# Two convolutions placed among the projection groups, with reordered work at three other places, in a one-core attention and FFN kernel

## The chip, the cores and the metric

The kernel runs on one core of one Trainium2 chip. The metric is device time in microseconds (us), the median of three runs. The core has a matrix engine (TensorE, PE in the profile; its weight loads are PEld), VectorE (DVE), ScalarE (ACT), GpSimd (POOL) and SyncE (SP), which here only issues DMAs. All operands come through SBUF, and matmul results land in PSUM, which has eight banks of 128 partitions x 512 float32.

## The reference

The input x has 32 batches of 64 channels x 1024. The reference computes, with everything in float32:

```python
x = x + attn(cond(x))          # cond: per-batch 64x64 mixing; attn: 32 batches of 64 rows, 32 heads, causal, plus a 10-row adapter
x = x + ffn(conv(x))           # conv: grouped, 9 taps along the 1024 axis, plus a context bias per batch
# ffn: base = xf @ W_base.T + b_base; top-2 router over 8 experts; rank-16 LoRA part added to base
```

In the reference the rows of attn's output and of ffn's input are the 2048 pairs (batch, channel), each of 1024 values. W_proj (in attn) and W_base (in ffn) are 1024 x 1024.

## The kernel before

Every large product is made of three matmuls that add up to float32 precision: each operand is split into a high part (ACT writes it, rounded) and a low part (DVE: value minus high part), and the passes are high x high, high x low and low x high. What the text calls a form is one operand in both parts: `high(G, f)` on ACT, then `low(G, f)` on DVE.

**Attention.** There are 32 units: 8 groups g of 128 output channels, 4 units u of 512 rows in each; n = 4g + u. In `unit_step`, PE projects K, Q and V (72 matmuls of 128x512), computes the scores of the unit before (L867), transposes, and multiplies with the values (L892, L898). DVE does the softmax of the unit before and rotates K and then Q (L1322 to L1329). ACT copies rotated K to `kbd` (four copies, L1196), then, where u is 0, the adapter's `akv` (L1207), then `aT` (L1131) and `pT` (L1134). In 16 of the units a slice of the weight forms of the later products is prepared as well: DVE subtracts blocks of the weights (`prep_sums`, four operations, L1388), ACT writes high parts (`prep_high`), DVE low parts (`prep_low`), and SP stores them. In before `prep_sums` stands ahead of the rotation of K.

**Groups 0 to 15.** NJ is 8. Groups G = 0 to 7 are the projection (W_proj), groups 8 to 15 the FFN; each handles two pairs of batches (t = 0, 1; 128 rows each). A group multiplies 256 rows by a 1024 x 1024 matrix in blocks of 512 with seven products instead of eight: `product(G, i)`, i = 0 to 6, twelve matmuls of 128x512 each. The operand forms are called, in the order of i, A11, S1, A22, S2, A12, S4, S3; S1 to S4 are sums of blocks that DVE makes (`add_up`). The results lie in four banks (A, C, D, B), and DVE and ACT combine them:

- `first_share` (ACT) copies product 0 to s1; `shares` (DVE) makes w12 and u2 from s1 and x, and adds product 1;
- `share21` adds product 2, `share12` adds product 3 to w12 (L1458); product 6 waits for `share12`, since it writes into the same bank B;
- `out11`, `out12` and `row2` write the two output rows into x1 (L1467 in the projection, L1464 in the FFN).

Between the products PE is in program order, and so are the other engines: each wait on a semaphore holds up everything behind it on its engine. The order of the work is written out by hand. Around the first group: product(0, 0) to (0, 5) are interleaved with the tail of unit 31; DVE's order of group 0 is shares, share21, low(1, A11), low(1, A22), share12(0) and so on, and those low parts need the attention output of the next pairs, `raw` (SP's `load_y(1)`, L689). `load_y(1)` stands on SP behind the store of the last unit's y (`store_y`, L660), which needs ACT's copy of it (`y_copy`), which needs the previous store to have landed; that store is queued behind three loads of weight forms.

**The turn to the FFN.** x1 of a projection group is written to DRAM (`put_aside`, L756). `spread(p)` (SP, L766, eight DMAs) reads it back in another layout into one of two buffers x8[p % 2], `load_ctx(p)` (L707) fetches the context bias, `convolve(p)` (PE, L999, 32 matmuls of 128x128) convolves into PSUM banks 0 and 1 (`bConv`), and `convolved(p)` (DVE, L1499) adds the bias and writes `raw` for FFN group 8 + p // 2. So convolve(0) and convolve(1) stand in group 7, and spread(2) and spread(3) can only start when their buffers have been read, in group 7 as well; convolve(2) and (3) stand in group 8. `load_x(8, t)` (L697) reads x1 of the first pairs back from DRAM for group 8, and POOL adds the base bias (`add_bias`, L841) into xn, which `shares(8)` needs. In the same stretch ACT issues the loads of the seven FFN weight forms, 2 MB each.

In the FFN, `hidden(G)` (L1015, L1017) computes router logits and LoRA rows, DVE does the routing (L1519 to L1542), PE transposes (L1025) and adds the LoRA part (`low_rank`, L1030). At the end `row2(15)` is two DVE operations, and one DMA of 512 KB stores them.

## Time and profile before

| | |
|---|---|
| median of 3 runs | 1206.33 us (1205.59 to 1206.85) |
| the profiled execution's own time | 1210.87 us |
| its span | 1208.8 us |
| PE busy | 1157.4 us, 96% |
| DVE busy | 924.1 us, 76% |
| ACT busy | 441.4 us, 37% |
| POOL busy | 54.3 us, 4% |

The span is that of one execution under the hardware profiler, and all times of day below are counted from its start. It is 2.1 us shorter than the execution's own time, which counts what lies around it. Attention runs to about 750 us, the projection groups to about 923 us, the FFN groups to the end. PE's idle time is small in total, and the profile tells for each piece what ended it.

### The profile page before, as it was taken

What the parts mean: (1) busy time and instruction counts of PE and PEld (TensorE: products, weight loads), DVE (VectorE), ACT (ScalarE), POOL (GpSimd) and SP (SyncE); (2) the same over time, 40 slices, a digit from 0 to 9 for tenths busy, and PEclk for the clock granted to TensorE, in tenths of its full rate; (3) what the DMA queues carried; (4) which work ended last, traced back from release to release, by engine and by line L of the source; (5) the groups of instructions that cost most, each with busy time, mean ns of one, the idle gap of its engine ahead of it and who ended that gap; (6) DMA issues with size and microseconds to landing.
All of it is one profiled execution on the core that took longest, in us unless ns stands there. A gap on an engine that the chain in (4) does not pass through costs nothing.

```text
span 1208.8 us, 19539 instructions
## 1 busy us (share of the span) xinstructions
PE 1157.4 (96%) x7568; PEld 974.1 (81%) x7568; DVE 924.1 (76%) x1741; ACT 441.4 (37%) x815; POOL 54.3 (4%) x25
## 2 busy tenths in 40 slices
PE   6999999999999999999999999799999499999998
PEld 5988878878878878878888877688888388888887
DVE  5887878878787787787887888678776177777775
ACT  4435354453543544535435446223221012221110
POOL 1000000000000000000000000000000122111122
PEclk9999999999999999999999999899999799999999
DMA  7413123033042041141232386674459533432312
GB/s 232 146 54 128 31 87 132 27 97 122 28 132 87 28 157 62 51 133 62 87 98 85 96 341 250 256 213 141 174 214 386 155 107 110 109 110 92 91 54 88
DMA packets 99465, 152.68 MB, mean 126 GB/s; under 512 B 7322, under 2 KB 83630, under 8 KB 96686
## 3 DMA queue, kind: packets, MB, share of 16 engines
q1 hardware_dynamic: 98366, 136.75, 35.0%
q10 hardware_dynamic: 1008, 14.68, 3.2%
q8 instruction: 61, 1.00, 0.3%
q14 instruction: 30, 0.25, 0.1%
HBM read 96.87 MB, written 54.54 MB: 125 GB/s over the span
## 4 chain that ended last, share of the span: by engine, by line
PE 53%; DVE 23%; issue 9%; ACT 7%; DMA 5%; SPq 3%; POOL 0%; DVEq 0%; ACTq 0%
PE psum L984 23%; PE psum L915 14%; PE psum L999 5%; ACT a_kbd L1196 3%; DVE a_stat L1347 2%; DVE a_prob L1362 2%; DVE a_prob L1343 2%; DVE a_stat L1358 2%; PE psum L260 2%; PE psum L898 2%; PE psum L1030 2%; SPq L766 2%; PE psum L1015 2%; PE psum L867 1%; DVE f_prep_raw L1388 1%
## 5 line engine op out<-in xcount | busy, mean ns | idle before, releaser
L915 PE MATMUL psum<-z,w_hi 128*128 128x512 f32 x1536 | 481.8, 395 | 0.0
L915 PEld LDWEIGHTS psum<-z,w_hi 128*128 128x128 f32 x1536 | 283.0, 188 | 55.3
L915 PE MATMUL psum<-z,w_lo 128*128 128x512 f32 x768 | 300.3, 391 | 0.0
L984 PE MATMUL psum<-f_wform,f_act_hi 128*128 128x512 f32 x896 | 280.5, 394 | 7.3 <-DVE f_w L1458 7.3
L984 PEld LDWEIGHTS psum<-f_wform,f_act_hi 128*128 128x128 f32 x896 | 167.1, 189 | 41.5 <-issue 7.7
L1196 ACT ACTIVATE a_kbd<-a_kr 32x512 f32<-32x512 f32 x128 | 80.7, 631 | 260.4 <-DVE a_kr L1329 259.3
L984 PE MATMUL psum<-f_wform,f_act_lo 128*128 128x512 f32 x448 | 175.3, 391 | 0.0
L915 PEld LDWEIGHTS psum<-z,w_lo 128*128 128x128 f32 x768 | 144.4, 188 | 30.8
L984 PEld LDWEIGHTS psum<-f_wform,f_act_lo 128*128 128x128 f32 x448 | 84.7, 189 | 18.0
L841 POOL TENSOR_TENSOR f_xn<-f_x,_bbase 128x1024 f32<-128x1024 f32 x16 | 49.6, 3097 | 1072.0 <-DMA f_x<-x_scratch 1072.0
L1166 ACT ACTIVATE f_act_hi<-f_raw 128x512 fp32r<-128x512 f32 x56 | 33.3, 626 | 142.0 <-DVE f_raw L1499 93.4
L1166 ACT ACTIVATE f_act_hi<-f_act_sum 128x512 fp32r<-128x512 f32 x64 | 40.2, 633 | 112.3 <-DVE f_act_sum L1420 45.3
L1426 DVE TENSOR_TENSOR f_act_lo<-f_raw,f_act_hi 128x512 fp32r<-128x512 f32 x56 | 37.2, 688 | 46.9 <-ACT f_act_hi L1166 46.9
L1343 DVE TENSOR_TENSOR a_prob<-psum,a_mask 128x512 f32<-128x512 f32 x64 | 43.8, 685 | 34.7 <-PE psum L867 34.7
L1124 ACT ACTIVATE a_prob<-a_prob 128x512 f32<-128x512 f32 x64 | 40.5, 633 | 65.1 <-DVE a_prob L1349 64.7
L1243 ACT ACTIVATE a_vbd<-psum 64x256 f32<-64x256 f32 x128 | 48.6, 380 | 25.8 <-PE psum L927 24.7
L1426 DVE TENSOR_TENSOR f_act_lo<-f_act_sum,f_act_hi 128x512 fp32r<-128x512 f32 x64 | 44.0, 689 | 14.0 <-ACT f_act_hi L1166 13.8
L1324 DVE STREAM_SHUFFLE a_rot<-psum 128x512 f32<-128x512 f32 x64 | 47.0, 735 | 0.0
L1349 DVE TENSOR_TENSOR a_prob<-a_prob,a_stat 128x512 f32<-128x512 f32 x64 | 44.3, 692 | 2.2
L1327 DVE TENSOR_TENSOR a_rot<-a_rot,a_sin 128x512 f32<-128x512 f32 x64 | 44.3, 692 | 2.2
L1362 DVE TENSOR_TENSOR a_prob<-a_prob,a_stat 128x512 f32<-128x512 f32 x64 | 44.3, 692 | 2.2
L1347 DVE TENSOR_REDUCE a_stat<-a_prob 128x8 f32<-128x512 f32 x64 | 43.9, 687 | 2.2
(173 smaller groups left out, 1583.2 us busy)
## 6 DMA issues: line engine op xcount, KB each, us to landing
w_forms<-f_prep_lo SPq DMA_DIRECT2D x16, 896.0 KB, 4.7
f_wform<-w_forms SPq DMA_DIRECT2D x7, 2048.0 KB, 12.7
f_wform<-w_forms ACTq DMA_DIRECT2D x7, 2048.0 KB, 16.3
w_st<-in_wqkvT SPq DMA_DIRECT2D x7, 1536.0 KB, 7.0
w_forms<-f_prep_hi SPq DMA_DIRECT2D x16, 640.0 KB, 6.0
m_x<-in_x SPq DMA_DIRECT2D x16, 512.0 KB, 4.0
y_scratch<-a_ysb SPq DMA_DIRECT2D x32, 256.0 KB, 2.4
f_raw<-y_scratch SPq DMA_DIRECT2D x8, 1024.0 KB, 6.1
```

The lines of the kernel that those rows point to most:

```text
L841: pool.tensor_tensor(xn[:, t, :].rearrange("p (m q) -> p q m", q=PH), x1[:, t, :].rearrange("p (q m) -> p q m", q=PH), bbase[:].rearrange( ...
L915: mm = pe.matmul(dst, w[:, c, x, :], zs, start=(c == 0 and i == 0), stop=(c == KC - 1 and i == 2))
L984: mm = pe.matmul(prod_bank[i][:], a[:, c, :], wform[i][:, w, c, :], start=(i < 4 and c == 0 and n == 0), stop=(c == KH - 1 and n == 2), sk ...
L999: mm = pe.matmul(bConv[:, o:o + P], x8[p % 2][:, CONV * b + g, j:j + P], toep[:, g, j, :], start=(j == 0), stop=(j == 1))
L1166: act.activation(act_hi[f][:], src, ACT.Copy).then_inc(act_hi_set, 1)
L1196: cp = act.activation(kbd[HD * h:HD * (h + 1), :, h % 2 * NC:(h % 2 + 1) * NC], kr[HD * h:HD * (h + 1), :].rearrange("p (b k) -> p b k", k ...
L1243: cp = act.activation(vbd[NC * h:NC * (h + 1), :, b, :, HD * h:HD * (h + 1)], bV[NC * b:NC * (b + 1), :].rearrange("p (s a h e) -> p s a h ...
L1324: dve.stream_shuffle(rot[:], src[:], HALF_SWAP).then_inc(turned[x], 1)
L1343: dve.tensor_tensor(prob[t][:].rearrange("p (s h) k -> p s h k", h=2), score_slots[:, UP * t:UP * (t + 1), 0:2 * NC].rearrange("p s (h k) ...
L1347: dve.tensor_reduce(stat[:, t, 0, :], prob[t][:], AX, ALU.max).then_inc(row_max, 1)
L1362: dve.tensor_tensor(prob[t][:], prob[t][:], spread(t, 2), ALU.mult).then_inc(probs, 1)
L1426: dve.tensor_tensor(act_lo[f][:], src, act_hi[f][:].bitcast(F32), ALU.subtract).then_inc(act_set, 1)
```

## The change

It has five parts, apart from names.

1. `prep_sums` moves from ahead of K's rotation to between the rotations of K and Q.
2. First group: ACT makes four of the seven high forms of group 0 ahead of the copy of V, one behind it and two behind the exponentials of the last unit. DVE leaves low(0, S4) and low(0, S3) to after share21(0), and in group 0 share12, out11 and out12 stand ahead of the low parts of group 1. SP issues load_y(1) and load_x(1, 1) ahead of the last store_y; load_y(1) has an additional wait for the four forms that still read `raw`.
3. convolve(0) stands at the start of group 5 and convolve(1) at the start of group 6. Pair 1 uses PSUM banks 2 and 3, and both results stay in PSUM until group 7, where `convolved(0)` and `(1)` stand as before. spread(2) is issued in group 5 and spread(3) in group 6.
4. POOL's add_bias for group 8 reads x1 right after group 0 has written it, so x1 isn't read back from DRAM for group 8. The writes to x1 in group 1 wait for POOL.
5. In group 15 the two products into bank B and the LoRA part of bank B are split into halves of 256 columns (the second in bank 0), and so are share12 and row2, and the last store.

```diff
@@ SP
             def load_y(G):
                 wait(sp, act_summed, 4 * G)
+                if G == 1:
+                    sp.wait_ge(act_set, 4)
...
             def spread(p):
-                load_ctx(p)
+                if p not in (2, 3):
+                    load_ctx(p)
...
-            store_y(NG - 1, NU - 1)
             def proj_group(G):
...
                 load_y(G + 1)
                 load_x(G + 1, 1)
                 if G == 0:
+                    store_y(NG - 1, NU - 1)
                     sp.wait_ge(y_out, 16 * NG * NU)
...
                 load_x(G + 1, 0)
+                if G in (NJ - 3, NJ - 2):
+                    spread(G - NJ + 5)
             def turn_group():
                 put_aside(G - 1, 1)
-                spread(2)
-                spread(3)
+                load_ctx(2)
+                load_ctx(3)
                 put_aside(G, 0)
-                load_x(G + 1, 0)
                 put_aside(G, 1)
-                load_x(G + 1, 1)
@@ POOL
             def add_bias(G, t):
-                pool.wait_ge(x_in[t], 16 * (G + 1))
+                if G == NJ and t == 0:
+                    pool.wait_ge(row1_set, 2)
+                elif G == NJ:
+                    pool.wait_ge(row2_set, 1)
...
@@ PE
             def convolve(p):
+                if p == 1:
+                    pe.wait_ge(y_copied, NG * NU)
...
-                wait(pe, conv_set, 2 * p)
+                wait(pe, conv_set, 2 * p if p >= 2 else 0)
...
             def hidden(G):
-                    pe.wait_ge(y_copied, NG * NU)
+                    pe.wait_ge(conv_set, 4)
...
             def group(G):
+                if G in (NJ - 3, NJ - 2):
+                    convolve(G - NJ + 3)
                 for i in range(4):
                     product(G, i)
-                if NJ - 1 <= G < 2 * NJ - 1:
+                if NJ <= G < 2 * NJ - 1:
                     convolve(2 * (G - NJ + 1))
@@ ACT
                 if n == NG * NU - 1:
-                    for f in form_order(0):
+                    for f in form_order(0)[:4]:
                         high(0, f)
                 (copy of V)
+                if n == NG * NU - 1:
+                    high(0, S2)
...
             attend_exp(m)
+            high(0, S4)
+            high(0, S3)
             first_share(0)
@@ DVE
             def out_half(G, t, half, src, other):
                 if ffn(G):
+                    if G == NJ:
+                        dve.wait_ge(x1_out[t], 16 * NJ)
...
                 wait(dve, x1_out[t], 16 * G)
+                if G == 1:
+                    dve.wait_ge(xn_set, t + 1)
...
             def unit_step(g, u):
-                if prep_at(n) is not None:
-                    prep_sums(prep_at(n))
                 rotate(K_, bK, kr, n, ((kbd_set, n),), n)
+                if prep_at(n) is not None:
+                    prep_sums(prep_at(n))
                 rotate(Q_, bQ, qr, n, ((scores, 2 * n),), n)
```

DVE in an attention unit with a weight slice (unit 5 of 32). a_kr and a_qr are rotated K and Q, f_prep_raw the weight blocks. Before:

```order
L1379 CAST a_aprob<-a_aprob 128x2x4x20
L1388 TENSOR_TENSOR f_prep_raw<-f_prep_raw 128x256 x4
L1322 TENSOR_TENSOR a_kr<-psum,a_cos 128x512
L1324 STREAM_SHUFFLE a_rot<-psum 128x512
L1327 TENSOR_TENSOR a_rot<-a_rot,a_sin 128x512
L1329 TENSOR_TENSOR a_kr<-a_kr,a_rot 128x512
L1322 TENSOR_TENSOR a_qr<-psum,a_cos 128x512
```

and now:

```order
L1408 CAST a_aprob<-a_aprob 128x2x4x20
L1351 TENSOR_TENSOR a_kr<-psum,a_cos 128x512
L1353 STREAM_SHUFFLE a_rot<-psum 128x512
L1356 TENSOR_TENSOR a_rot<-a_rot,a_sin 128x512
L1358 TENSOR_TENSOR a_kr<-a_kr,a_rot 128x512
L1417 TENSOR_TENSOR f_prep_raw<-f_prep_raw 128x256 x4
L1351 TENSOR_TENSOR a_qr<-psum,a_cos 128x512
```

The four block sums have changed places with K's rotation; Q's rotation stands where it stood.

DVE in group 0, from share21(0) on. f_u_85 is u2, f_w_84 is w12, f_x_126 is x1, f_act_lo_64 to 70 are the low parts of A11, S1, A22, S2, A12, S4, S3, f_act_sum_73 is the sum S1. Before:

```order
L1453 TENSOR_TENSOR f_u_85<-psum,f_u_85 128x512
L1426 TENSOR_TENSOR f_act_lo_64<-f_raw,f_act_hi_56 128x512
L1426 TENSOR_TENSOR f_act_lo_66<-f_raw,f_act_hi_58 128x512
L1458 TENSOR_TENSOR f_w_84<-psum,f_w_84 128x512
L1412 TENSOR_TENSOR f_act_sum_73<-f_raw 128x512
L1415 TENSOR_TENSOR f_act_sum_75<-f_act_sum_73,f_raw 128x512
L1426 TENSOR_TENSOR f_act_lo_65<-f_act_sum_73,f_act_hi_57 128x512
L1467 TENSOR_TENSOR f_x_126<-psum,f_xt_81 128x64x8
```

and now:

```order
L1482 TENSOR_TENSOR f_u_85<-psum,f_u_85 128x512
L1455 TENSOR_TENSOR f_act_lo_69<-f_act_sum_77,f_act_hi_61 128x512
L1455 TENSOR_TENSOR f_act_lo_70<-f_act_sum_78,f_act_hi_62 128x512
L1492 TENSOR_TENSOR f_w_84<-psum,f_w_84 128x512
L1505 TENSOR_TENSOR f_x_126<-psum,f_xt_81 128x64x8
L1505 TENSOR_TENSOR f_x_126<-psum,f_w_84 128x64x8
L1455 TENSOR_TENSOR f_act_lo_64<-f_raw,f_act_hi_56 128x512
L1455 TENSOR_TENSOR f_act_lo_66<-f_raw,f_act_hi_58 128x512
L1441 TENSOR_TENSOR f_act_sum_73<-f_raw 128x512
L1444 TENSOR_TENSOR f_act_sum_75<-f_act_sum_73,f_raw 128x512
L1455 TENSOR_TENSOR f_act_lo_65<-f_act_sum_73,f_act_hi_57 128x512
```

share12(0) and both outputs of the first row have moved ahead of all work on the next pairs' `raw`, and the last two low parts of group 0 have moved in behind share21.

SP from group 6 to the first FFN group. _x_95 and f_x_next are the two convolution buffers, f_ctxb the context biases, x_scratch is x1 in DRAM. Before:

```order
L756 DMA x_scratch<-f_x_126 128x1024 x2
L707 DMA f_ctxb_134<-ctx_scratch 128x128
L766 DMA _x_95<-x_scratch 16x8x128 x8
L707 DMA f_ctxb_135<-ctx_scratch 128x128
L766 DMA f_x_next<-x_scratch 16x8x128 x8
L756 DMA x_scratch<-f_x_126 128x1024
L697 DMA f_x_126<-x_scratch 128x1024
L756 DMA x_scratch<-f_x_126 128x1024
L697 DMA f_x_126<-x_scratch 128x1024
```

and now:

```order
L771 DMA _x_95<-x_scratch 16x8x128 x8
L760 DMA x_scratch<-f_x_126 128x1024 x2
L694 DMA f_raw<-y_scratch 128x2x1024
L707 DMA f_xt_82<-in_x 128x1024
L707 DMA f_xt_81<-in_x 128x1024
L771 DMA f_x_next<-x_scratch 16x8x128 x8
L760 DMA x_scratch<-f_x_126 128x1024 x2
L711 DMA f_ctxb_134<-ctx_scratch 128x128
L711 DMA f_ctxb_135<-ctx_scratch 128x128
L760 DMA x_scratch<-f_x_126 128x1024 x2
```

The sixteen gathers for pairs 2 and 3 have moved one group and more ahead, and the two loads of x1 (L697) at this place are gone.

## Rows read from the trace of the kernel before

**Rows 1.** The page, parts 1 and 2: PE's row and its granted clock.

```profile
PE 1157.4 (96%) x7568; PEld 974.1 (81%) x7568; DVE 924.1 (76%) x1741; ACT 441.4 (37%) x815; POOL 54.3 (4%) x25
...
PEclk9999999999999999999999999899999799999999
```

**Rows 2.** Waits of PE: line, releaser, us in total, times, longest.

```profile
PE psum L999 <- DVE f_raw L1499: 10.9, 1, 10.9
PE psum L984 <- DVE f_w L1458: 7.3, 1, 7.3
PE psum L999 <- DMA _x<-x_scratch: 7.1, 1, 7.1
PE psum L898 <- ACT a_pT L1134: 4.6, 8, 0.6
...
PE psum L905 <- ACT a_akv L1207: 2.8, 7, 0.4
PE psum L892 <- ACT a_aT L1131: 2.8, 7, 0.6
...
PE psum L927 <- ACT a_vT L1232: 0.8, 1, 0.8
```

**Rows 3.** Timeline of PE, 908 to 972: start, duration, idle time before.

```profile
908.15 3.73 PE L999 MATMUL psum<-_toep,_x 128*128 128x128 f32 x32
...
945.72 5.89 PE L999 MATMUL psum<-_toep,_x 128*128 128x128 f32 x32 [7.14 <-DMA _x<-x_scratch]
...
965.25 6.33 PE L999 MATMUL psum<-_toep,f_x_next 128*128 128x128 f32 x32 [10.88 <-DVE f_raw L1499]
```

**Rows 4.** Timeline of SP and of DVE in the same stretch.

```profile
922.42 21.23 SPq L766 DMA_DIRECT2D f_x_next<-x_scratch  x8
...
956.63 0.69 DVE L1435 TENSOR_TENSOR f_w<-f_s,f_xn 128x512 f32<-128x512 f32 x1 [22.04 <-POOL f_xn L841]
```

**Rows 5.** The page, part 6: DMA issues, KB each, us to landing.

```profile
f_wform<-w_forms ACTq DMA_DIRECT2D x7, 2048.0 KB, 16.3
...
out<-f_x SPq DMA_DIRECT2D x16, 512.0 KB, 3.1
```

**Rows 6.** Timeline of PE, 777 to 784.

```profile
777.90 1.19 PE L984 MATMUL psum<-f_wform,f_act_hi 128*128 128x512 f32 x2 [7.29 <-DVE f_w L1458]
...
783.01 0.63 PE L984 MATMUL psum<-f_wform,f_act_hi 128*128 128x512 f32 x2
```

**Rows 7.** Chain of waits, 740 to 1209: start, duration, what.

```profile
751.09 16.89 DMA y_scratch<-a_ysb
...
769.17 5.95 DMA f_raw<-y_scratch
```

**Rows 8.** Chain of waits, 1190 to 1209: the last product.

```profile
1201.66 2.75 PE psum L984 x12
```

**Rows 9.** Timeline of DVE, 775 to 780: first and last of six operations.

```profile
775.86 1.30 DVE L1426 TENSOR_TENSOR f_act_lo<-f_raw,f_act_hi 128x512 fp32r<-128x512 f32 x2 [10.78 <-ACT f_act_hi L1166]
...
779.12 0.69 DVE L1426 TENSOR_TENSOR f_act_lo<-f_act_sum,f_act_hi 128x512 fp32r<-128x512 f32 x1
```

**Rows 10.** Timeline of DVE, 932 to 934 and 1187 to 1191.

```profile
932.98 0.87 DVE L1535 TENSOR_SCALAR f_we<-_iota,f_rs 128x8 f32<-128x8 f32 x4
...
1187.02 3.68 DVE L1535 TENSOR_SCALAR f_we<-_iota,f_rs 128x8 f32<-128x8 f32 x4
```

**Rows 11.** Timeline of POOL at the second of these places.

```profile
1187.12 3.16 POOL L841 TENSOR_TENSOR f_xn<-f_x,_bbase 128x1024 f32<-128x1024 f32 x1 [1.46 <-DMA f_x<-x_scratch]
```

**Rows 12.** Timeline of PE: the scores of units 12, 13 and 14.

```profile
333.89 1.24 PE L867 MATMUL psum<-a_kbd,a_qr 64*64 64x148 f32 x32
355.91 1.24 PE L867 MATMUL psum<-a_kbd,a_qr 64*64 64x148 f32 x32
376.72 1.24 PE L867 MATMUL psum<-a_kbd,a_qr 64*64 64x148 f32 x32
```

**Rows 13.** Timeline of DVE: the block sums of one weight slice.

```profile
696.10 1.68 DVE L1388 TENSOR_TENSOR f_prep_raw<-f_prep_raw 128x256 f32<-128x256 f32 x4
```

More of the change, by code:

```diff
@@ L1557, in first_forms @@
                 add_up(0, S3)
[L1558 removed]
+                for f in (A11, S1, A22, A12, S2):
                     low(0, f)
[L1560 to L1563 removed]
             def unit_step(g, u):
@@ L1621, in group @@
                     share21(G)
-                if G < NJ - 1:
+                if G == 0:
+                    low(0, S4)
+                    low(0, S3)
+                    share12(0)
+                    out11(0)
+                    out12(0)
+                    for f in (A11, A22):
+                        low(1, f)
+                    add_up(1, S1)
+                    add_up(1, S2)
+                    low(1, S1)
+                    low(1, A12)
+                    add_up(1, S4)
+                    low(1, S2)
+                    low(1, S4)
+                elif G < NJ - 1:
                     low(G + 1, A11)
@@ L1660, in group @@
                     share21(G)
-                    row2(G)
+                    for part in range(2):
+                        cols = slice(HALF // 2 * part, HALF // 2 * (part + 1))
+                        dve.wait_ge(prod, NPROD * G + 7 + part)
+                        dve.wait_ge(u21_set, G + 1)
+                        dve.tensor_tensor(x1[:, 1, :].rearrange("p (s n) -> p s n", s=2)[:, :, cols],
+                                          (bB, bank[0])[part][:, cols].rearrange("p (s n) -> p s n", s=1)
+                                          .broadcast_to([P, 2, HALF // 2]), u2[:, :, cols], ALU.add).then_inc(row2_set, 1)
                 if G == 1:
```

63 lines of the change are left out of this document (38 added, 25 removed).

## The prediction

> **What bounds the kernel now.** I read the page first: TensorE (PE) is busy for 96% of the span [rows 1], so only three things can make the kernel faster: less idle time of PE, fewer matmuls, or a higher granted clock where it is low. The clock row has dips in two places only, at 0.8 and 0.7 of full speed. I then read the list of PE's waits, which has few entries of size [rows 2]: 10.9 and 7.1 us at the entry of the FFN, 7.3 us in the first projection group, and 4.6 + 2.8 + 2.8 us in many small pieces in the attention. Then the timeline around each, for what the wait costs beyond its idle time. Both clock dips belong to these waits: the matmuls behind them run at half rate. The 32 small matmuls of a convolution take 3.73 us at the full clock, and 5.89 and 6.33 us behind the two FFN waits; a product of twelve takes 2.75 us [rows 8], and 783.01 - 777.90 = 5.11 us behind the third [rows 3, 6]. In the profile's rows the granted clock is 0.5 there, the lower of the two levels (1.2 GHz), after an idle stretch, and 1.0 (2.4 GHz) again after a few us of work. No matmul of size is removed, so the change is worth what it takes from these stretches, less what it adds.
>
> **Part 3 and 4, the entry of the FFN.** Today the second buffers' gathers wait for convolutions 0 and 1 in group 7, and their eight issues for pair 3 alone stretch over 21.23 us, beside 14 MB of weight forms (16.3 us to landing each) [rows 4, 5]. So x8 for pair 2 lands late (7.14 us idle), the reload of x1 stands behind it on SP, POOL's bias add behind that, and DVE waits 22.04 us for xn; with DVE late, convolution 3 finds its PSUM banks still full (10.88 us idle) [rows 3, 4]. The change moves the gathers of pairs 2 and 3 into groups 5 and 6 and drops the reload. Both chains are cut at their head. What goes: 7.14 + (5.89 - 3.73) + 10.88 + (6.33 - 3.73) = 22.8 us.
>
> What is late next? Convolutions 0 and 1 no longer stand in group 7, which loses 2 x 3.73 = 7.5 us of cover, but groups 5 and 6 gain the same, so PE's sum is unchanged. Counted from the start of group 7: hidden(8) can start after seven products, 7 x 2.75 = 19.2 us. The convolution results lie ready, and DVE takes them after share12, so after four products, at about 11 us. Eight DVE operations of 0.7 us at most [rows 9] and ACT's copies between them lead to all four plain forms: about 18 us, and the last of these is needed only by the second half of hidden(8). It fits by one to three us. The weight forms are asked for by ACT as each product of group 7 ends, so seen from group 8 they come earlier by the two convolutions that stood between the products, except the last two, which follow the forms of group 8; they have half a group and more. I cost this at 0, and 5 us if the cover fails. The new gathers in groups 5 and 6 stand behind that group's loads on SP, in front of put_aside, and the same eight issues already stand in groups 1 and 2, where no wait of PE is listed. Part: 22.8 us, between 17 and 23.
>
> **Part 2, the first group.** PE's 7.29 us before product(0, 6) end with share12(0), which stands on DVE behind low parts that need load_y(1); that was held by two y stores one behind the other (16.89 us for the first) and then takes 5.95 us [rows 6, 7]. share12 now stands ahead of that work, so product(0, 6) follows product(0, 5) at once: 7.29 + (5.11 - 2.75) = 9.65 us. Three high forms fewer stand ahead of the copy of V, whose wait is 0.8 us [rows 2]. Together 10.5 us.
>
> Now load_y(1). It is issued at about 751 and no longer behind the last store. The first store, queued behind the three weight forms, landed at 751.09 + 16.89 = 768.0; load_y(1) stands right behind it in the same queue, so it lands between 769 and 774. product(0, 5) ended at 777.90 - 7.29 = 770.6, now 769.8; out12(0) follows, about 1.1 us, and the low parts can start at 770.9. product(1, 0) would start at 769.8 + 2.75 = 772.55 and product(1, 1) at 775.3. From the first low part to the end of low(1, S1) before took 779.81 - 775.86 = 3.95 us with share12 among them [rows 9], so some 3.35 now: 774.3. With nothing in between, all is in time.
>
> But there is something in between: the end of out12(0) now also releases POOL's bias add, and the end of row2(0) the second. How POOL and DVE get along is in the trace: the same four small DVE operations take 0.87 us alone and 3.68 us when a bias add of POOL (3.16 us) runs at their start [rows 10, 11]. A DVE operation with two operands in SBUF stands still for the length of POOL's, 2.8 us more. The Trainium skill (SBUF — State Buffer, "SBUF: two separate sides") has the rule: the port pair that VectorE and GpSimd share is locked for a whole instruction and not divided; by it each add costs DVE its full 3.16 us if POOL gets the lock first, nothing if DVE keeps it. The trace agrees with the first as far as it goes. low(1, A11) and its followers are such operations, so 774.3 becomes 777.1 and product(1, 1) waits about 2 us. The second add sits just ahead of add_up(1, S3), and that is what load_y(2) waits for: its landing (6 us and more), then two high and low parts and share12(1), which again stands behind those low parts in group 1, must be done for product(1, 6) at 769.8 + 7 x 2.75 = 789. Counting it through, load_y(2) goes out at about 782, lands at 788 to 790, and share12(1) ends at 791 to 793, against a product moved by the first wait to about 791. I take 3.5 us for both, between 0 and 7. Part: 10.5 - 3.5 = 7.0 us, between 3.5 and 10.5. No clock dip behind waits this short: the 0.4 to 0.6 us ones show none, longer ones are open, and the bound holds it.
>
> **Part 1, the block sums.** The small attention waits are for ACT: akv, aT and pT are copied behind the four kbd copies, and these start when DVE has rotated K. The four sums that stood ahead take 1.68 us [rows 13]. Moved behind, K is rotated 1.6 us earlier and so are all of ACT's copies, against waits of 0.4 to 0.6 us. Q's rotation ends where it ended, so the scores lose nothing, and DVE, which afterwards waited for ACT's high parts of the slice, waits less. A unit with such a wait takes 355.91 - 333.89 = 22.02 us, the next one without 376.72 - 355.91 = 20.81, so 1.21 each [rows 12]. With seven aT waits: 7 x 1.21 = 8.5; the eighth pT wait about 1.0; the seven akv waits 2.8. Part: 12.3 us, between 10.2 (the bare idle time) and 13.
>
> **Part 5, the tail.** Two DVE operations behind the last matmul become one, 0.6 us less. Half of a 512 KB store (3.1 us [rows 5]) remains: between 0 and 1.5 less, I take 0.4, since two small transfers still have a start and a landing. Against it stand 24 matmuls of 256 columns for 12 of 512, twice, and 6 for 3. No row shows that width; the bounds are 3.73 / 32 = 0.117 us at 128 columns and 2.75 / 12 = 0.229 at 512, which make 0.1 and 6.2 us for all of it. Because 0.117 at a quarter of the width says that it is set by loading weights, I take 0.12 at half: 0.3 us. Part: 0.7 us, between -5 and +1.5.
>
> **Sum.** 22.8 + 7.0 + 12.3 + 0.7 = 42.8 us. The profiled execution, 1210.87 us with 1208.8 us of span, would become 1168.1; it lies 4.5 us above the median of the runs, and I take the difference to the median: 1206.33 - 42.8 = 1163.5 us.
>
> **The rivals.**
> - *POOL does no harm.* DVE keeps the port through its run of operations, or load_y(2) lands early. For it: DVE has few gaps there. Against: rows 10 show that POOL gets in. All parts at their upper value: 22.8 + 10.5 + 13 + 1.2 = 47.5, so 1158.8 us.
> - *A new wait at the turn.* The 7.5 us of cover taken from group 7 are missed: DVE has not made the forms when hidden(8) could start, or a weight form lands late, and PE idles long enough for the clock to fall again. For it: the margin of one to three us. Against: the last form's need is late in the group. 5 us idle and 2.4 of slow matmuls: 1171 us.
> - *The rotation order brings little*, because ACT's copies are held by something else behind the same wait (transposes, the copy of y). Against: the trace has ACT idle until rotated K in each unit. 3 us in place of 12.3: 1173 us.
> - *Slower than before.* The clock, which returned in 5 us after the gaps, stays at its lower level for long in the now denser projection stretch. A product then costs 5.11 - 2.75 = 2.36 us more; from 18 of the 112 products on it eats the whole gain, and at 25 the time is 1222 us. Against: hundreds of us of attention without a gap run at the full clock [rows 1].
> - *It doesn't do what it says*: convolution 1 or 2 waits for another semaphore of the same chain. Against: all that they wait for is set groups earlier. It would bring back 7 to 12 us: 1173.
>
> **How the numbers follow.** The forecast has a chance of 0.57, with its own range of 1160.5 to 1166.5; POOL harmless 0.15; a wait at the turn 0.12; little from the rotations 0.08; the last 0.05; slower 0.03. Below 1158.5 there is nearly nothing, since all that could be taken is taken there; the upper end at 1171 takes in the wait at the turn and leaves out the last three in part. A measurement of this kernel can tell about 0.2% from no change, 2.4 us: faster by more 0.96, within 0.01, slower 0.03.
>
> **What would show it.** In the profile after: no wait of PE at L999's successor (convolution 2 and 3), and convolutions of 3.7 us throughout; the scores of u = 1 units 20.8 us apart and no akv, aT and pT rows among PE's waits; product(0, 6) right behind product(0, 5); a wait of PE of about 2 us in the first products of group 1, for a low part of DVE beside a POOL operation, and one of about 1.5 us at product(1, 6) for share12. A PE wait at the first hidden product or at a product of group 8, a fall of the granted clock after 770 us, or a time outside 1158.5 to 1171 would prove the forecast wrong.

## The result, and the profile after

| | before | after |
|---|---|---|
| median of the runs | 1206.4 us (1205.59 to 1206.85, 4 runs) | 1162.1 us (1160.39 to 1165.66, 4 runs) |
| ratio to before | | 0.9637 (95%: 0.9614 to 0.9661) |
| the profiled execution's own time | 1210.87 us | 1160.39 us |
| its span | 1208.8 us | 1158.6 us |

The time fell by 44.3 us, against 42.8 forecast. The page of the changed kernel, the rows that answer to [rows 1]:

```profile
PE 1141.3 (99%) x7595; PEld 964.7 (83%) x7595; DVE 926.9 (80%) x1742; ACT 442.2 (38%) x815; POOL 55.2 (5%) x25
...
PEclk9999999999999999999999999999999999999999
```

Both dips of the granted clock are gone. The list of PE's waits (line, releaser, us in total, times, longest) answers to [rows 2]; lines have moved, L984 is L1001 now and L999 is L1019:

```profile
PE psum L225 <- DMA m_mlp<-in_mlp: 3.2, 1, 3.2
PE psum L260 <- DVE f_z_raw L342: 2.5, 1, 2.5
PE psum L1001 <- DVE f_act_lo L1455: 1.8, 1, 1.8
PE psum L236 <- DVE m_att_wide L312: 1.7, 1, 1.7
PE psum L260 <- DMA m_x<-in_x: 1.4, 1, 1.4
PE psum L881 <- DVE a_avs L1631: 1.1, 1, 1.1
PE psum L1001 <- DVE f_u L1474: 0.8, 1, 0.8
```

No row names a convolution, pT, aT or akv. What is left lies before the first scores, at 67 us, but for two rows that before did not have: 1.8 us for a low part and 0.8 us for u, both in group 1.

The two traces are compared stretch by stretch, since the start differs by 5.1 us although nothing was changed there (it took 66.9 to 72.9 us over all traces of this study, and its waits for the loads of x differ each time). The stretches are cut where PE starts a known piece: the first score matmul of unit 0, the last one of unit 31, the first hidden product of group 8, and the transposes of the hidden products of group 8 (first) and 15 (last). So "turn" is the tail of unit 31 with groups 0 to 7, "hidden(8)" runs from the hidden products of group 8 to their transposes, and "FFN" reaches from there to group 15. The cut points are read to 0.1 us, so a difference of 0.1 between two stretches means nothing. Some expectations below cut at the first score matmul of unit 31, which makes attention 0.9 us shorter (662.3 here), and at the first transpose of group 15, which makes the tail 0.1 us longer. Times in us:

| | start | attention | turn | hidden(8) | FFN | tail | span |
|---|---|---|---|---|---|---|---|
| before | 72.3 | 677.2 | 174.0 | 14.7 | 254.9 | 15.7 | 1208.8 |
| after | 67.2 | 663.2 | 166.5 | 14.7 | 232.0 | 15.0 | 1158.6 |

The parts gave 14.0 (attention), 7.5 (first group, in "turn"), 22.9 (FFN entry) and 0.7 (tail): 45.1 us together. The convolutions of the FFN entry, once 5.89 and 6.33 us behind waits of 7.14 and 10.88 [rows 3], in the timeline of PE after:

```profile
911.84 3.73 PE L1019 MATMUL psum<-_toep,_x 128*128 128x128 f32 x32
918.16 3.74 PE L1019 MATMUL psum<-_toep,f_x_next 128*128 128x128 f32 x32
```

The forecast had also named a place for a new cost. These are DVE, POOL and PE in groups 0 and 1 (start, duration, and in brackets the idle time before and what ended it):

```profile
751.47 4.20 DVE L1455 TENSOR_TENSOR f_act_lo<-f_raw,f_act_hi 128x512 fp32r<-128x512 f32 x2
...
764.32 2.81 DVE L1455 TENSOR_TENSOR f_act_lo<-f_act_sum,f_act_hi 128x512 fp32r<-128x512 f32 x1 [0.76 <-ACT f_act_hi L1191]
```

```profile
751.80 3.33 POOL L855 TENSOR_TENSOR f_xn<-f_x,_bbase 128x1024 f32<-128x1024 f32 x1 [688.22 <-DVE f_x L1505]
763.12 3.47 POOL L855 TENSOR_TENSOR f_xn<-f_x,_bbase 128x1024 f32<-128x1024 f32 x1 [7.99 <-DVE f_x L1505]
```

```profile
757.77 0.73 PE L1001 MATMUL psum<-f_wform,f_act_hi 128*128 128x512 f32 x2 [1.83 <-DVE f_act_lo L1455]
...
769.75 0.69 PE L1001 MATMUL psum<-f_wform,f_act_hi 128*128 128x512 f32 x2 [0.77 <-DVE f_u L1474]
```

Two low parts take 1.28 us without company; beside POOL's add they took 4.20, and one took 2.81 in place of 0.69. DVE lost 2.9 and 2.1 us.

### The profile page after: what moved, and what is told of

The parts are those of the page before. It is cut to its first block, busy times and chain, and to the rows that moved or that the text cites. A ratio compares the mean times of both kernels' runs of the same rounds, so it can differ in the third digit from the quotient of the medians.

```text
span 1158.6 us, 19585 instructions
## 1 busy us (share of the span) xinstructions
PE 1141.3 (99%) x7595; PEld 964.7 (83%) x7595; DVE 926.9 (80%) x1742; ACT 442.2 (38%) x815; POOL 55.2 (5%) x25
## 4 chain that ended last, share of the span: by engine, by line
PE 96%; DVE 2%; issue 1%; ACT 0%; DMA 0%; DVEq 0%; ACTq 0%
PE psum L929 45%; PE psum L1001 25%; PE psum L1019 5%; PE psum L881 3%; PE psum L912 3%; PE psum L897 2%; PE psum L1053 2%; PE psum L260 2%; PE psum L1035 2%; PE psum L941 2%; PE psum L950 1%; PE psum L890 1%; PE psum L1037 1%; PE psum L906 1%; DVE z L353 1%
## 5 line engine op out<-in xcount | busy, mean ns | idle before, releaser
L1001 PE MATMUL psum<-f_wform,f_act_hi 128*128 128x512 f32 (+1 forms) x912 | 279.7, 389 | 2.6 <-DVE f_act_lo L1455 1.8
L1001 PEld LDWEIGHTS psum<-f_wform,f_act_hi 128*128 128x128 f32 x912 | 167.9, 188 | 36.4 <-DVE f_act_lo L1455 2.3
L1001 PE MATMUL psum<-f_wform,f_act_lo 128*128 128x512 f32 (+1 forms) x456 | 176.0, 386 | 0.0
L1001 PEld LDWEIGHTS psum<-f_wform,f_act_lo 128*128 128x128 f32 x456 | 85.7, 188 | 17.6
L1455 DVE TENSOR_TENSOR f_act_lo<-f_raw,f_act_hi 128x512 fp32r<-128x512 f32 x56 | 40.1, 740 | 29.5 <-ACT f_act_hi L1191 29.5
L1455 DVE TENSOR_TENSOR f_act_lo<-f_act_sum,f_act_hi 128x512 fp32r<-128x512 f32 x64 | 46.1, 722 | 13.8 <-ACT f_act_hi L1191 13.8
L1378 DVE TENSOR_TENSOR a_prob<-a_prob,a_stat 128x512 f32<-128x512 f32 x64 | 44.3, 692 | 2.2
L1356 DVE TENSOR_TENSOR a_rot<-a_rot,a_sin 128x512 f32<-128x512 f32 x64 | 44.3, 692 | 2.2
L1391 DVE TENSOR_TENSOR a_prob<-a_prob,a_stat 128x512 f32<-128x512 f32 x64 | 44.3, 692 | 2.2
```

Source lines behind the costliest of these rows:

```text
L1001: mm = pe.matmul((prod_bank[i], bank[0])[part][:, cols], a[:, c, :], wform[i][:, w, c, cols], start=(i < 4 and c == 0 and n == 0), stop=(c ...
L1356: dve.tensor_tensor(r, r, tab[1], ALU.mult).then_inc(rot_step, 1)
L1378: dve.tensor_tensor(prob[t][:], prob[t][:], spread(t, 0), ALU.subtract).then_inc(shifted, 1)
L1391: dve.tensor_tensor(prob[t][:], prob[t][:], spread(t, 2), ALU.mult).then_inc(probs, 1)
L1455: dve.tensor_tensor(act_lo[f][:], src, act_hi[f][:].bitcast(F32), ALU.subtract).then_inc(act_set, 1)
```

## The experiments

Each kernel is the changed one with one edit. The stretches of all of them, with the ratio of the runs to the kernel before on the same chip:

| kernel | attention | turn | FFN | tail | ratio (95%) |
|---|---|---|---|---|---|
| after | 663.2 | 166.5 | 232.0 | 15.0 | 0.9637 (0.9614 to 0.9661) |
| 1 sums ahead | **677.0** | 166.6 | 231.9 | 15.0 | 0.9749 (0.9731 to 0.9767) |
| 2 adds late | 663.2 | **168.6** | 232.0 | 15.0 | 0.9640 (0.9615 to 0.9664) |
| 3 reload | 663.2 | **163.2** | **251.2** | 15.0 | 0.9754 (0.9726 to 0.9783) |
| 4 convolutions in 7 | 663.2 | 166.4 | **242.2** | 15.1 | 0.9690 (0.9662 to 0.9717) |
| 5 share12 behind | 663.2 | **168.2** | 231.9 | 15.1 | 0.9644 (0.9623 to 0.9666) |
| 6 store first | 663.2 | **168.5** | 232.0 | 15.0 | 0.9648 (0.9627 to 0.9670) |
| 7 tail whole | 663.2 | 166.9 | 231.7 | **15.7** | 0.9647 (0.9624 to 0.9671) |
| 8 convolutions in 7, reload | 663.2 | 166.8 | **255.2** | 15.1 | one run, 1189.1 us |
| 9 add twice | 663.2 | **170.5** | 231.9 | 15.1 | 0.9664 (0.9640 to 0.9688) |
| 10 late adds, share12 ahead | 663.2 | **169.1** | 232.0 | 15.0 | 0.9657 (0.9635 to 0.9679) |
| 11 ScalarE copies | 663.2 | 166.6 | 231.9 | 15.1 | 0.9630 (0.9608 to 0.9653) |
| 12 ScalarE copies, gathers held | 663.2 | **163.3** | 231.9 | 15.1 | **0.9590 (0.9573 to 0.9608)** |

A stretch that no edit touches repeats to within 0.5 us, and mostly 0.1, where medians of runs scatter by 1 to 3 us. So the smaller effects are read from the stretches, each from one trace. The kernels ran on several chips, each beside the kernel before, so the ratios are the fair comparison between them.

### 1. The block sums

```
-                rotate(K_, ...)
                 if prep_at(n) is not None:
                     prep_sums(prep_at(n))
+                rotate(K_, ...)
```

> The changed kernel with one thing undone: the four block sums of a weight slice stand on VectorE ahead of K's rotation again. Theory (K's rotation 1.7 us earlier lets all of ACT's copies start earlier, and PE waits for these): the akv, aT and pT rows of 0.4 to 0.6 us come back among PE's waits, the stretch from the scores of unit 0 to those of unit 31 grows from 662.3 to 676 us, the time by 12 to 14 us, to about 1176. Rival A (the copies are held by something else, and the attention gained through another part of the change): under 3 us, about 1164. Rival B (half of the attention's gain is of the order in the last unit and not of the sums): 6 to 8 us, about 1169.

Attention grew by 13.8 us and no other stretch moved; the difference of the ratios is 1.1%, or 13.5 us. The rows are back:

```profile
PE psum L912 <- ACT a_pT L1159: 4.6, 8, 0.6
...
PE psum L906 <- ACT a_aT L1156: 2.8, 8, 0.4
PE psum L919 <- ACT a_akv L1232: 2.6, 7, 0.4
```

The theory holds. The waits are 10.0 us of idle time, but cost 13.8; the starts of the scores in one group of units show where. First this kernel, then the changed one:

```profile
216.89 1.24 PE L881 MATMUL psum<-a_kbd,a_qr 64*64 64x148 f32 x32
240.76 1.24 PE L881 MATMUL psum<-a_kbd,a_qr 64*64 64x148 f32 x32
262.88 1.24 PE L881 MATMUL psum<-a_kbd,a_qr 64*64 64x148 f32 x32
```

```profile
215.18 1.24 PE L881 MATMUL psum<-a_kbd,a_qr 64*64 64x148 f32 x32
238.60 1.24 PE L881 MATMUL psum<-a_kbd,a_qr 64*64 64x148 f32 x32
259.36 1.24 PE L881 MATMUL psum<-a_kbd,a_qr 64*64 64x148 f32 x32
```

The unit with the akv wait takes 23.87 against 23.42 us (0.45 more), the one with the aT and pT waits 22.12 against 20.76 (1.36 more, for 1.0 us of idle time). This group is the dearest of the seven: in the others the aT and pT waits are 0.9 us together and the unit takes 22.0 us, 1.23 to 1.26 more. The unit behind it, which has no wait, takes about 20.82 against 20.76.

### 3, 4 and 8. The FFN entry: gathers, or reload?

Kernel 3 loads x1 for group 8 again, and POOL adds the bias to it there and no longer in groups 0 and 1:

```
+                    sp.wait_ge(x1_out[t], 16 * NJ)
...
                 put_aside(G, 0)
+                load_x(G + 1, 0)
                 put_aside(G, 1)
+                load_x(G + 1, 1)
```

> The changed kernel with part 4 undone alone: the first pair of the FFN is loaded again from x_scratch behind the last put_aside, and GpSimd adds the bias then and not in groups 0 and 1; the gathers of pairs 2 and 3 stay in groups 5 and 6. Theory (the late gathers were the head of both chains, so the reload comes in time once they are gone; in the first groups no GpSimd instruction disturbs VectorE): waits of 1.83 and 0.77 us in group 1 gone, 0 to 2 us of waits before the convolutions 2 and 3 at the FFN entry, the time 0 to 2.6 us below the changed kernel, about 1161. Rival (the reload is by itself late, since it stands behind put_aside of group 7): VectorE waits 10 us and more for xn in group 8 and PE 8 to 13 us before convolution 3, about 1172.

Kernel 4 puts spread(2) and (3) and convolve(0) and (1) back into group 7:

```
-                if G in (NJ - 3, NJ - 2):
-                    spread(G - NJ + 5)
...
-                if G in (NJ - 3, NJ - 2):
-                    convolve(G - NJ + 3)
...
-                if NJ <= G < 2 * NJ - 1:
+                if NJ - 1 <= G < 2 * NJ - 1:
```

> The changed kernel with part 3 undone alone: gathers and convolutions of pairs 2 and 3 (the first two of the FFN) in group 7 again, in the banks 0 and 1 both; the pair that GpSimd reads is still not loaded again. Theory (the gathers stand behind put_aside of group 6 beside 14 MB of weight forms, and land late): PE waits 7 us before the first hidden product and runs the convolution behind it at half rate, 9.3 us more; the 10.9 us wait before convolution 3 stays away, since VectorE has xn long before; about 1171.5. Rival (the gathers alone made both waits, VectorE being late through the convolution results and not through xn): 20 to 23 us more, about 1184.

Kernel 8 has both edits; there is one execution of it.

> The changed kernel with parts 3 and 4 undone together, which closes the square: so far the FFN stretch (transposes of group 8 to those of group 15) was 232.0 us with both, 251.2 with the early gathers alone, 242.2 with the dropped reload alone, and 254.9 in the kernel before. Theory (nothing outside the two parts acts on this stretch): 254.5 to 255.5, and 163.2 from last scores to first hidden product. Rival (the tighter attention and first group shift the transfers at the turn): off by more than 1.5 us either way.

The FFN stretch is 232.0 with both parts, 242.2 without the early gathers, 251.2 without the dropped reload, 255.2 with neither (254.9 in before, so within 0.3 us nothing else acts here). For the turn the expectation of kernel 8 failed: it is 166.8 us and not 163.2, with a wait of 3.1 us for share12(1), which the part on kernels 11 and 12 takes up. In kernel 4 the theory held in size; the wait stands before convolution 2 in group 8, not before the hidden products as the expectation says:

```profile
924.49 6.05 PE L1014 MATMUL psum<-_toep,_x 128*128 128x128 f32 x32 [7.78 <-DMA _x<-x_scratch]
933.12 3.74 PE L1014 MATMUL psum<-_toep,f_x_next 128*128 128x128 f32 x32
```

7.78 + (6.05 - 3.73) = 10.1 us. In kernel 3 my theory fell, and the rival held in kind, with a wait longer than its 8 to 13 us:

```profile
937.34 6.15 PE L1017 MATMUL psum<-_toep,f_x_next 128*128 128x128 f32 x32 [16.68 <-DVE f_raw L1531]
```

With the gathers long done, convolution 3 waits 16.68 us, longer than before, and with its slow matmuls costs 19.1. SP and POOL show why; the first two lines are the store of one half of x1 and its reload:

```profile
902.63 0.32 SPq L761 DMA_DIRECT2D x_scratch<-f_x  x1
915.04 0.32 SPq L702 DMA_DIRECT2D f_x<-x_scratch  x1
915.41 0.43 SPq L761 DMA_DIRECT2D x_scratch<-f_x  x1
926.88 0.32 SPq L702 DMA_DIRECT2D f_x<-x_scratch  x1
```

```profile
925.91 2.85 POOL L853 TENSOR_TENSOR f_xn<-f_x,_bbase 128x1024 f32<-128x1024 f32 x1 [856.63 <-DMA f_x<-x_scratch]
930.23 2.86 POOL L853 TENSOR_TENSOR f_xn<-f_x,_bbase 128x1024 f32<-128x1024 f32 x1 [1.47 <-DMA f_x<-x_scratch]
```

The store takes 12.4 us to land and the reload 10.7, where such stores and reloads have a median of 3.5 us each over this kernel. The DMA view from 902 to 926 (queue, packets, MB, share of the 16 engines) has the queue of the weight forms, q10, ahead of SP's, q1:

```profile
q10 hardware_dynamic: 569, 8.23, 80.2%
q1 hardware_dynamic: 595, 1.63, 16.9%
```

The reload of the second half is the counterpart: issued at 926.88, when the weight forms have landed, it takes 3.3 us, and the DMA view from 926.8 to 930.5 has one queue only:

```profile
q1 hardware_dynamic: 144, 0.52, 46.3%
```

So the reload is late by itself, behind its store and beside the weight forms, and the gathers' chain ran for the most part in its shadow: the early gathers alone bring 3.7 us, the dropped reload alone 12.7, both 22.9.

### 5 and 6. The first group: DVE's order, or SP's?

Kernel 5 puts share12(0), out11(0) and out12(0) back among the parts for group 1; kernel 6 puts the last store of y ahead of load_y(1) again.

```
                 if G == 0:
                     low(0, S4)
                     low(0, S3)
-                    share12(0)
-                    out11(0)
-                    out12(0)
...
-                elif G < NJ - 1:
+                if G < NJ - 1:
```

> The changed kernel with VectorE's order in group 0 undone alone: share12(0) stands behind the low parts of A11 and A22 of group 1 again, and out11 and out12 between the later sums; the load of y for group 1 keeps its new place ahead of the last store of y. Theory (the early load does part of the work by itself: it has landed at 750.7, so the low parts end at 753.1 and share12 at 753.8): PE waits 3 to 4 us before the seventh product of group 0 without a fall of the clock, of which the wait of 1.83 us in group 1 is given back; 1.5 to 2.5 us slower than the changed kernel, about 1164. Rival A (the order was the whole cure): the wait of 7.3 us and the slow product behind it return, 9 to 10 us slower, about 1171.5. Rival B (GpSimd's adds, released later by out12, do less harm): no difference, 1162.

```
+            store_y(NG - 1, NU - 1)
             def proj_group(G):
...
                 if G == 0:
-                    store_y(NG - 1, NU - 1)
```

> The changed kernel with SP's order at the end of the attention undone alone: the last store of y stands ahead of the load of y for group 1 again; VectorE keeps share12 ahead of the low parts. Theory (the load is then issued at about 749 behind that store in the queue): the seventh product of group 0 follows the sixth at once, but the first product of group 1 waits 3 to 7 us for its low part, and the product behind it runs at half rate if the wait is long enough: 4 to 8 us slower, about 1168. Rival A (VectorE's order alone was the cure, the load comes in time either way): within 1 us, 1162. Rival B (the load queues behind the store and the weight forms as before and lands near 768): 12 us and more slower, about 1175.

Kernel 5 waits 3.28 us before product(0, 6), as the theory said, and has no wait for the low part in group 1 any more; the turn grows by 1.7 us. In kernel 6 the low parts of group 1 come at 760.43, behind a load issued at 753.91; PE waits 3.46 us, and matmuls at half rate follow (two in 1.05 us in place of 0.62), 1.7 us lost on them:

```profile
761.18 0.75 PE L1001 MATMUL psum<-f_wform,f_act_hi 128*128 128x512 f32 x2 [3.46 <-DVE f_act_lo L1455]
...
763.43 1.05 PE L1001 MATMUL psum<-f_wform,f_act_hi 128*128 128x512 f32 x2
```

That is 5.2 us, within the 4 to 8 of the theory. The turn grows by only 2.0, because I had not taken off what the changed kernel loses in group 1, 3.2 us (kernel 12), and what this one does not lose a second time. Against the waitless turn of 163.3 us the cost is 3.2 us with both orders, 4.9 and 5.2 with either one alone, and 10.7 with none (before). Each alone saves most of what the two save together. The 10.7 hold 0.8 us for the copy of V [rows 2]; that wait is gone in all the kernels here, and no run puts ACT's order back alone.

### 2, 9 and 10. What POOL's adds cost

Kernel 9 does the first add twice; kernels 2 and 10 release the adds only behind group 1's shares, kernel 10 with share12(1) ahead of the low parts for group 2 as well.

```
 # 9                for again in range(2 if G == NJ and t == 0 else 1): ...
 # 2, 10            pool.wait_ge(row1_set, 2)
+                   pool.wait_ge(u22_set, 2)
```

> The changed kernel with the first of GpSimd's bias adds done twice, one behind the other (the result is the same). Theory (the port pair is VectorE's or GpSimd's for the whole instruction): VectorE loses about 3 us more in the first low parts and sums of group 1, PE's wait of 1.83 us there becomes 4.5 to 5.2 us, the stretch from last scores to first hidden product 169 to 170 us; 2.5 to 3.3 us slower than the changed kernel, about 1165. Rival (VectorE keeps the port once it has it and the second add waits for a gap between its instructions): the second add starts late, PE's wait grows by under 1 us, 1162 to 1163.

> The changed kernel, and GpSimd's first bias add (and so the second, behind it) also waits for the second u22 share, the last of group 1's shares: both adds leave the stretch in which PE waited 1.83 us before the second and 0.77 us before the sixth product of group 1. Theory (the two waits are the price of the shared port, 2.9 and 2.1 us on VectorE): both waits go, the low parts of A11 and A22 of group 1 take 1.28 us in place of 4.20 and that of S3 0.69 in place of 2.81; the adds now fall on the low parts of group 2 or on VectorE's wait for the load of y, at most 1 us lost there; 1.5 to 2.6 us faster than the changed kernel, about 1160. Rival A (the waits are the chain through ACT's high parts and the sums, GpSimd or not): no change, 1162. Rival B (the adds do the same harm wherever they stand, since share12 of group 1 stands behind the low parts): waits of 2 to 3 us at the seventh product of group 1 or at the first of group 2, 1162 to 1163.

> The other candidate: GpSimd's first adds behind the shares of group 1, as in the run with the late adds, and in addition share12 of group 1 ahead of the low parts for group 2, as group 0 has it. Theory (in the run with late adds PE waited 3.6 us for share12 alone, which stood behind low parts whose y landed at 771): that wait goes, what is left is a wait of 0 to 2.5 us at the first products of group 2, since their low parts still hang on that load and on GpSimd's lock; the stretch from last scores to first hidden product 163.5 to 166, 1159.5 to 1162. Rival (the late load of y is the bound whatever stands ahead): a wait of 3 us and more in group 2, stretch 166.5 or more, 1162 to 1163.

Kernel 9: POOL's two adds run from 753.63 for 6.76 us, DVE's next operations take 4.19 and 3.34 us, and PE waits 4.65 us in place of 1.83. The matmuls behind the wait run at half rate, which costs 2.5 us more. The turn is 4.0 us longer, 170.5 against the 169 to 170 expected:

```profile
753.47 4.19 DVE L1462 TENSOR_TENSOR f_act_lo<-f_raw,f_act_hi 128x512 fp32r<-128x512 f32 x2
757.59 3.34 DVE L1448 TENSOR_TENSOR f_act_sum<-f_raw 128x512 f32<-128x512 f32 x1
```

The theory holds here: at a place where DVE has no slack the second add of POOL is paid nearly in full. But kernel 2 did not get faster. Both waits are gone and DVE's low parts take 1.29 us, yet PE waits 3.59 us for share12(1) (f_w), and 1.7 us go to slow matmuls behind it:

```profile
765.67 0.68 DVE L1483 TENSOR_TENSOR f_u<-psum,f_u 128x512 f32<-128x512 f32 x1
771.84 1.29 DVE L1456 TENSOR_TENSOR f_act_lo<-f_raw,f_act_hi 128x512 fp32r<-128x512 f32 x2 [5.49 <-ACT f_act_hi L1192]
773.05 0.68 DVE L1493 TENSOR_TENSOR f_w<-psum,f_w 128x512 f32<-128x512 f32 x1
```

DVE stands for 5.49 us waiting for ACT, which waits for the next y. Counted from out12(0) in each, that load was issued 2.5 us earlier than in the changed kernel, and ACT could begin 1.2 us later. Kernel 10 removes the wait for share12(1) only to wait 2.96 us for out11(1) (f_x) before the first product of group 2, behind the same load and the late add, with 2.9 us lost on slow matmuls. So its rival holds. In kernel 2 the wait has the place that rival B named, but not its reason: the adds ran while DVE stood idle.

### 11 and 12. A faster kernel

ACT, 38% busy, copies x1 to xn in groups 0 and 1, and POOL adds the bias in place in groups 4 and 5, where DVE waits for y.

```
+            def copy_pair(t):
+                act.wait_ge(row2_set if t else row1_set, 1 if t else 2)
+                act.activation(xn[:, t, :]..., x1[:, t, :]..., ACT.Copy).then_inc(xn_copied, 1)
...
+                    pool.wait_ge(xn_copied, t + 1)
+                    pool.wait_ge(u21_set, 5 + t)
+                    pool.tensor_tensor(xn[:, t, :], xn[:, t, :], bbase[:], ALU.add).then_inc(xn_set, 1)
```

> A candidate better than both: the changed kernel, but ScalarE copies the first FFN pair from x1 to xn in groups 0 and 1 (two copies, in its idle time of 4.5 and 3.3 us there), and GpSimd adds the bias in place later, in groups 4 and 5, released when VectorE comes to its wait for the next load of y; nothing is loaded again. Theory (the 3.3 us of group 0 and 1 are what GpSimd's two adds take from VectorE at a place without slack, and where VectorE waits anyway they cost nothing): the stretch from the last scores to the first hidden product falls from 166.5 to 163.2 us, no wait of PE in groups 1, 4 and 5, the FFN stretch stays at 232; 1.5 to 3.3 us faster than the changed kernel, about 1159.3. Rival A (the copies take ScalarE's time where the high parts need it): 166 or more, 1162. Rival B (an add costs VectorE's chain 3 us in groups 4 and 5 as well, and PE waits there): 166 to 169, 1162 to 1165.

The turn stayed at 166.6. The adds in groups 4 and 5 cost PE nothing and the copies (2.18 and 2.20 us of ACT) next to nothing, but the wait for share12(1) is there again, 2.86 us. So neither rival was it: with POOL out of the way, the load of y for group 2 is the bound. From the issue of that load to ACT's first high part from it, over the traces: 5.6 to 6.1 us in the seven with the disturbed DVE (changed kernel and kernels 1, 4, 5, 6, 7, 9), 9.3, 8.9, 8.8 and 8.8 in kernels 2, 8, 10 and 11, and 5.6 in kernel 3. In the slow ones, and in kernel 3, SP issued the next load of x 3.2 us behind it, as DVE's shares came sooner, and the eight gathers right after; in the seven 5.3 us behind, when it had nearly landed. Kernel 12 is kernel 11 with SP waiting for the landing first:

```
                 load_y(G + 1)
+                if G in (1, 2):
+                    sp.wait_ge(y_in, 16 * (G + 2))
                 load_x(G + 1, 1)
```

> The kernel in which ScalarE copies the first FFN pair, and in addition SP lets the load of y for groups 2 and 3 land before it issues the next load of x, the context load and the eight gathers. So far, where GpSimd left VectorE alone, that load was issued 3.5 us earlier and in four of five traces took 8.8 to 9.3 us until ScalarE could begin (5.6 in the fifth), against 5.6 to 6.1 in the seven traces with GpSimd's adds, in which the other transfers were issued 5.3 us and not 3.2 us behind it. Theory (the transfers behind it in the queue share the engines with it and push its landing back): 5.6 to 6.0 us in this kernel, no wait of PE in group 1, the stretch from last scores to first hidden product 163.2 to 163.6 us, 3 us less than the changed kernel, about 1159. Rival (it is slow because of what was ahead of it or by its early place, whatever follows): 8.8 us again, PE waits about 3 us for share12 of group 1, the stretch stays at 166.6, 1162.

```profile
760.38 0.37 SPq L695 DMA_DIRECT2D f_raw<-y_scratch  x1
766.01 0.33 SPq L708 DMA_DIRECT2D f_xt<-in_x  x1
```

```profile
766.08 1.15 ACT L1195 ACTIVATE f_act_hi<-f_raw 128x512 fp32r<-128x512 f32 x2 [2.42 <-DMA f_raw<-y_scratch]
```

5.7 us, no wait of PE in group 1, and the turn 163.3. The median is 1159.3 us (1156.87 to 1159.90, 5 runs), and the interval of the ratio, 0.9573 to 0.9608, lies below that of the changed kernel, 0.9614 to 0.9661. It is faster than before and than the changed kernel, over the latter by 3.2 us in the stretches, 2.8 in the medians and 0.47% in the ratios. Against kernel 11, whose interval is 0.9608 to 0.9653, the two intervals only touch.

What the wait on SP did to the landing rests on one trace each, and the traces give two reasons for care. Kernels 3 and 8 have the same instructions up to group 4, with 3.2 us between the two issues in both, and the load took 5.6 us in one and 8.9 in the other. And the next load of y, for group 3, has the same transfers 3.2 us behind it in every trace but kernel 12's: it took 5.5 to 7.7 us there, and 6.1 in kernel 12. So with the same instructions the landing varies between executions by more than 3 us. That holding back the later transfers keeps it short fits all traces, and the faster runs speak for it, but that it is the cause of the 5.7 us is not shown.

### 7. The tail

```
-            for part in range(2): ... # two DVE operations and two stores of 256 columns
+            store_out(2 * NJ - 1, 1)
...
-                parts = 2 if G == 2 * NJ - 1 and prod_bank[i] is bB else 1
+                parts = 1
```

The LoRA part of bank B, share12 and row2 are whole again as well.

> The changed kernel with part 5 undone alone: the last low-rank products and the last product with 512 columns in one bank, one last pair of VectorE operations on all of row 2 and one store. Theory (a 256-column matmul takes 0.12 us, half of the 512; the end loses one VectorE operation and half a store): the stretch from the last turn of the hidden products to the end of the span grows from 15.2 to 15.8 us, the time by 0.4 to 0.8 us. Rival (the difference of the two traces at the tail was scatter): under 0.2 us, or below.

The tail is 15.7 against 15.0 us, as in before. The runs (0.9647 against 0.9637, intervals overlapping) can't tell it from nothing; the traces agree with the theory, and the tail of every other trace with the split is within 0.1 us of the 15.0. In the chain of waits of the changed kernel, against [rows 8], the last 24 matmuls of 256 columns are

```profile
1152.08 2.88 PE psum L1001 x24
```

which is 0.12 us each, against 2.75 us for 12 of 512 columns.

## Why the prediction was right, and where it was not

- **FFN entry: 22.8 forecast, 22.9 measured.** The sum was right since both parts were made. The step "both chains are cut at their head", with the gathers as the head, was wrong: the reload needed no late gathers ahead of it to be late itself (kernel 3, 16.68 us of wait). I read the wait of 22.04 us [rows 4] back through SP's queue to the gathers and stopped at the first cause; that the store and the reload of 512 KB are slow while the weight forms are loading (10.7 us, and 3.3 once they have landed, in kernel 3) I did not ask.
- **First group: 7.0 forecast (10.5 less 3.5), 7.5 measured.** From the last scores to product(1, 0) the gain is 10.8 us, and 3.3 are given back, as kernel 12 shows by taking them out. The first wait came where it was forecast (1.83 us for a low part beside POOL's add). The second came one product earlier and for u, 0.77 us, not for share12, so that 3.3 came so near to 3.5 is in part luck. No slow matmul followed either, as assumed. The chain that I had counted for share12 was there too, hidden behind POOL: it came out in kernels 2, 8 and 11, with waits of 3.6, 3.1 and 2.9 us.
- **POOL and the port.** Rows of DVE and POOL at the same instant show DVE standing still for nearly as long as POOL's add lasts, in kernel 9 twice in a row. What the Trainium skill states (SBUF — State Buffer, "SBUF: two separate sides"), a lock for the whole instruction, agrees with the 4.20 us against 1.28, and with the 3.34 against 0.68. "POOL does no harm" would not have given its 1158.8 for sure either: without the harm the load of y asked the same price or more in four traces of five, and only the fifth (kernel 3) had the turn of 163.2 us without a wait on SP.
- **Block sums: 12.3 forecast, 14.0 measured** (13.8 by kernel 1), above the bound of 13. The mechanism was right and the term was mis-sized in small pieces. Against the changed kernel the units of before with an akv wait took 0.46 to 0.49 us more, not the 0.4 of the bare wait (0.5 us in sum). Those with aT and pT waits took 1.23 to 1.27 more, not 1.21, since the unit behind that I took as the reference, 20.81 us, was itself slowed a little (20.76 now), and one of them took 1.52 more (0.6 us in sum). That slowing of units without a wait is itself 0.5 us more, and the last pT wait gave 1.1 us and not 1.0.
- **Tail: 0.7 forecast, 0.7 measured in the stretch.** The 256-column matmul took the 0.12 us that I had chosen between 0.117 and 0.229. Against kernel 7 the last DVE work is 0.6 us shorter, as forecast, and what follows it 0.2 us (0.4 forecast for the store). The matmuls cost 0.1 us in the tail and 0.15 in product(15, 3), which lies ahead of the cut. The whole part is therefore worth 0.5 us, and the exact agreement of 0.7 owes something to the place of the cut.
- **Next to be late at the turn: nothing.** hidden(8) starts without a wait, and the granted clock is 1.0 from 770 us to the end.

The forecast of 42.8 us was 1.5 too small by the medians and 2.3 by the stretches, of which the block sums are 1.7.

## What to carry to other kernels

When two chains overlap, the longer one hides much of the other: undoing one part of a change at a time shows each part's price only given the other (3.7 or 10.2 us for the gathers, 12.7 or 19.2 for the reload). A wait that goes away by removing its releaser's delay may be replaced at the same size by the next chain, and an engine that becomes faster makes transfers go out earlier, and perhaps into each other's way. Here the kernel that turned the freed time into speed also had one wait on SP, which holds back transfers that are not urgent. Compare traces by stretches between fixed points of the program, since start-up differs from one execution to the next by more than most edits are worth.

## What was not expected of the hardware

- The landing of one and the same load varies, and may depend on what is queued behind it: the 1 MB of y for group 2 took 5.6 to 6.1 us when the next transfers were issued 5.3 us later, 8.8 to 9.3 in four of five traces of the changed kernels when they were issued 3.2 us later (7.9 in before), and 5.7 when they were held. The fifth (kernel 3, 5.6 us at 3.2 us distance) and the load for group 3 (5.5 to 7.7 at that distance) show that the overlap alone does not make the delay.
- POOL's add is slower beside DVE too: the same add took 2.85 us with DVE idle (kernel 3), 3.33 and 3.47 with DVE at work (changed kernel). In place and with plain addressing it took 2.40 and 2.70 in kernel 11; DVE lost 0.5 and 2.2 us beside them, and PE nothing.
- Idle times of PE of 2.86 and 3.28 us (kernels 11 and 5) were followed by matmuls at a granted clock of 1.0, those of 3.46, 3.59 and 4.65 us (kernels 6, 2 and 9) by some at 0.5, which lost 1.7, 1.7 and 2.5 us more; but so was one of 2.96 us (kernel 10: two matmuls in 1.06 us and not 0.62, 2.9 us lost). So the length of the idle time alone does not tell in this range whether the clock falls.
